# Two orders and one place of work in a two-layer transformer kernel: score matmuls of layer 0, ScalarE's and TensorE's steps of layer 1, statistics of twelve tiles

## The reference

```
ada = silu(c) @ W_ada + b_ada            # six rows: shift, scale, gate, twice
h = layernorm(x) * (1 + scale_msa) + shift_msa
x = x + gate_msa * (attention(h) @ W_proj + b_proj)
h = layernorm(x) * (1 + scale_mlp) + shift_mlp
x = x + gate_mlp * (gelu(h @ W_fc1 + b_fc1) @ W_fc2 + b_fc2)
```

## Time and profile before

| | |
|---|---|
| median of the runs | 905.08 us (904.79 to 906.73) |
| the profiled execution | 905.91 us, its span 904.1 us |
| granted TensorE clock over the span | 0.972 |
| busy, share of the span | PE 87%, DVE 72%, ACT 58%, POOL 31% |

### The profile page before, as it was taken

How to read it: one execution, slowest core, us unless ns; L and a number is a source line. 1 busy time by engine, 2 the same in 40 slices (tenths; PEclk the granted TensorE clock), 3 DMA queues, 4 the chain that set the end, 5 groups by cost and what they waited for, 6 DMA issues and landing times. The chain is left out here.

```text
span 904.1 us, 16521 instructions
## 1 busy us (share of the span) xinstructions
PE 788.5 (87%) x6096; PEld 364.0 (40%) x6096; DVE 647.4 (72%) x1277; ACT 525.0 (58%) x731; POOL 281.0 (31%) x369
## 2 busy tenths in 40 slices
PE   1568989999998989899898999999979875999996
PEld 0234222222222222222234465566646553666564
DVE  4849788888887898888935955656686898834521
ACT  4433477676676676776785725635557634535630
POOL 4320011325554241102023437241233465421122
PEclk9979799999999999999999999999999996999999
DMA  7302010110111100000040011101676710000000
GB/s 222 78 21 73 20 28 27 28 47 12 40 44 47 47 27 21 21 21 21 2 109 2 11 41 40 31 9 60 149 190 167 171 36 27 7 1 28 26 26 27
DMA packets 52127, 45.35 MB, mean 50 GB/s; under 512 B 23898, under 2 KB 41236, under 8 KB 52055
## 3 DMA queue, kind: packets, MB, share of 16 engines
q1 hardware_dynamic: 47613, 36.35, 15.7%
q10 hardware_dynamic: 4442, 8.04, 2.8%
HBM read 27.66 MB, written 9.46 MB: 41 GB/s over the span
## 5 line engine op out<-in xcount | busy, mean ns | idle before, releaser
L956 DVE TENSOR_REDUCE row_max<-ps 128x1 f32<-128x512 f32 x512 | 322.6, 686 | 62.1 <-PE ps L1682 61.2
L1445 ACT ACTIVATE probs<-ps 128x1024 f32<-128x1024 f32 x256 | 249.0, 1018 | 57.0 <-PE ps L1709 56.3
L1682 PE MATMUL ps<-stack_area 54*128 54x512 f16 x512 | 150.5, 389 | 27.9 <-DVE row_max L956 21.3
L1721 PE MATMUL ps<-probs,mlp_area 128*32 128x512 f32 x1024 | 138.0, 611 | 0.0
L1709 PE MATMUL ps<-stack_area 56*128 56x512 f16 x512 | 110.7, 385 | 7.2 <-ACT probs L1445 7.2
L1682 PEld LDWEIGHTS ps<-stack_area 54*128 54x128 f16 x512 | 37.1, 93 | 192.7 <-DVE row_max L956 174.0
L1855 PE MATMUL ps<-w_fc,mlp_area 128*128 128x288 f16 x864 | 107.7, 286 | 4.7 <-DVE mlp_area L1097 4.7
L1834 PE MATMUL ps<-mlp_area,w_fc 128*128 128x512 f16 x504 | 110.8, 379 | 0.8 <-ACT mlp_area L1486 0.8
L1486 ACT ACTIVATE mlp_area<-ps 128x512 f32<-128x512 f32 x72 | 42.8, 595 | 98.0 <-PE ps L1834 95.5
L1855 PEld LDWEIGHTS ps<-w_fc,mlp_area 128*128 128x128 f16 x864 | 83.8, 98 | 27.4 <-DVE mlp_area L1097 3.9
L765 POOL TENSOR_SCALAR neg_scaled<-neg_max 128x16 f32<-128x16 f32 x16 | 4.0, 253 | 279.8 <-DVE neg_max L963 279.8
(11 more groups left out here) (170 smaller groups left out, 1098.6 us busy)
## 6 DMA issues: line engine op xcount, KB each, us to landing
stack_area<-tokens SPq DMA_DIRECT2D x124, 36.0 KB
qkv_rows<-part_area ACTq DMA_DIRECT2D x14, 252.0 KB
qkv_rows<-probs ACTq DMA_DIRECT2D x10, 252.0 KB
x_sb<-in_x SPq DMA_DIRECT2D x4, 576.0 KB, 7.4
w_raw<-in_L_cond_W_fc SPq DMA_DIRECT2D x4, 576.0 KB
tokens<-qkv_rows SPq DMA_DIRECT2D x64, 36.0 KB
v_sb<-qkv_rows SPq DMA_DIRECT2D x16, 144.0 KB
w_raw<-in_L_cond_fc_w SPq DMA_DIRECT2D x4, 576.0 KB
```

The lines of the kernel that those rows point to most:

```text
L956: nc.vector.reduce_max(row_max[:, p % 2, t, j, half:half + 1], bank(bk), AX.X).then_inc(max_done, 1)
L1445: nc.scalar.activation(probs[:, n % 2, 2 * c:2 * c + 2, :].rearrange("p h n -> p (h n)"), ps[:, 2 + 2 * c:4 + 2 * c, :].rearrange("p b n - ...
L1682: nc.tensor.matmul(bank(bk), stacks[rows, p % RING, 0, t * P:(t + 1) * P], stacks[rows, p % RING, 1, half * 512:(half + 1) * 512], start=T ...
L1721: mm = nc.tensor.matmul(bank(6)[at:at + VW, :], v_pad[:, TB * (p // BPAIR) + n, 2 * (p % BPAIR) + j, :], probs[:, n % 2, 2 * c + j, :], st ...
```

## The change

Three things are altered.

Layer 0: in each slot TensorE follows a list, `PE_ORDER`. A P group is now cut 1-2, 3, 4-5, 6-7 and its last three pieces stand behind S1 and O: weigh, P 1-2, S0, S1, O, P 3 to 7, A, S2, B, S3. The four S steps, P and O keep their order in `plan_banks`. B's two matmuls start with the second head (`SCORE_HEADS`). The waits ahead of the first scores stand at the start of slot -1 instead of its middle.

Layer 1's attention: in ScalarE's step the columns, `high_attention` and `high_part` come before `widen` and the exponent, and the weight job before `take_rows`. In VectorE's step `invert_sums(k-1)` comes before `subtract_maxima(k)`, and `low_attention` and `turn_v` come last. In TensorE's step `out_mms` and the turned tiles come before `cell_scores`.

Statistics of layer 1's middle: those of tiles 0 to 3 stay in the steps; those of 4 to 7 stand behind step 18 between the last projections; those of 8 to 15 stand in chunk 0 of the MLP, two behind each `fc2_y`. GpSimd's `invert` follows them, and its waits on them in the steps leave.

```diff
@@ -395,6 +395,9 @@
         SCORES_FIRST = -1
+        PE_ORDER = ['W', 'P0', 'S0', 'S1', 'O', 'P1', 'P2', 'P3', 'A', 'S2', 'B', 'S3']
+        PART_RANGES = [(0, 2), (2, 3), (3, 5), (5, 7)]
+        SCORE_HEADS = [(0, 1), (1, 0)]
 
@@ -441,7 +444,8 @@
                 maxima, others = maxima_of(s), other_of(s)
-                for i, step in enumerate(part_of(s) + maxima[:2] + others + maxima[2:]):
+                order = [x for k in PE_ORDER for x in (part_of(s) if k == 'P0' else maxima[int(k[1]):int(k[1]) + 1] if k[0] == 'S' else others if k == 'O' else [])]
+                for i, step in enumerate(order):
                     now = s + i / 6
@@ -850,7 +854,8 @@
                         for t in OUT_AT.get(k - 2, ()):
-                            pool.wait_ge(rstd_ready, 3 * NT + t + 1)
+                            if t < PT_:
+                                pool.wait_ge(rstd_ready, 3 * NT + t + 1)
                         if k > 1:
@@ -860,12 +865,12 @@
                         for t in OUT_AT.get(k - 1, ()):
-                            invert(t, 3 * NT + t)
-                    for t in range(TB, NT + 2):
-                        if t < NT:
-                            add_projection(1, t)
-                        if t > TB + 1:
-                            invert(t - 2, 3 * NT + t - 2)
+                            if t < PT_:
+                                invert(t, 3 * NT + t)
+                    for t in range(TB, NT):
+                        add_projection(1, t)
+                    for t in range(PT_, TB):
+                        invert(t, 3 * NT + t)
                 stats = 2 * NT * l + NT
@@ -880,6 +885,11 @@
                 add_mlp(0)
+                if l:
+                    for t in range(TB, NT):
+                        invert(t, 3 * NT + t)
+                        if t % 2 and t < NT - 1:
+                            add_mlp(t // 2 - 3)
                 if l == 0:
@@ -889,7 +899,7 @@
                                           ).then_inc(pads_set, 1)
-                with pool.Fori(1 if l else 4, NT) as t:
+                with pool.Fori(4, NT) as t:
                     add_mlp(t)
@@ -1109,6 +1119,9 @@
                                                        fc2_bias[:], ALU.mult, ALU.add).then_inc(fc2_y, 1)
+                        if l and isinstance(c, int) and c == 0:
+                            mid_statistics(TB + 2 * i)
+                            mid_statistics(TB + 2 * i + 1)
                     if l == 0 and isinstance(c, int) and i in JOBS_AT_FC2.get(c, ()):
@@ -1180,24 +1193,25 @@
                         turn_cells(k - 2)
+                    if 0 < k <= NSTEP:
+                        invert_sums(k - 1)
                     if k < NSTEP:
                         subtract_maxima(k)
-                    if 0 < k <= NSTEP:
-                        invert_sums(k - 1)
-                    if k > 2:
-                        low_attention(k - 3)
+                    for t in OUT_AT.get(k - 1, ()):
+                        if t < PT_:
+                            mid_statistics(t)
                     for t in TILES_AT.get(k - 1, ()):
                         low_part(0, t % 2, NT + t)
                     for t in TILES_AT.get(k, ()):
                         normalise(0, t, t % 2, NT + t, 2 * NT + t, t // TB, 0)
-                    for i, a in TURN_V_AT.get(k, ()):
-                        turn_v(i, a)
-                    for t in OUT_AT.get(k - 1, ()):
-                        mid_statistics(t)
                     for t in OUT_AT.get(k, ()):
                         take_projection(1, t, t % 2, t < 2)
                     if k in JOB_STEPS:
                         low_weights(JOB_STEPS[k])
+                    if k > 2:
+                        low_attention(k - 3)
+                    for i, a in TURN_V_AT.get(k, ()):
+                        turn_v(i, a)
 
@@ -1248,10 +1262,9 @@
                             take_projection(1, TB + i - 2, i % 2, False)
-                    for t in range(TB + 2, NT + 2):
-                        mid_statistics(t - 2)
-                        if TB + 4 <= t < NT:
-                            take_projection(1, t, t % 2, False)
+                    for t in range(PT_, TB):
+                        take_projection(1, TB + t, t % 2, False)
+                        mid_statistics(t)
                 if l == 0:
@@ -1382,20 +1395,20 @@
                 for k in range(NSTEP + 3):
+                    for t in TILES_AT.get(k - 2, ()):
+                        take_columns(t, t % 2)
+                    if k > 2:
+                        high_attention(k - 3)
+                    for t in TILES_AT.get(k - 1, ()):
+                        high_part(0, t % 2, NT + t, 2)
                     if 1 < k < NSTEP + 2:
                         widen(k - 2)
                     if k < NSTEP:
                         exponents_of_cells(k)
-                    if k > 2:
-                        high_attention(k - 3)
-                    for t in TILES_AT.get(k - 1, ()):
-                        high_part(0, t % 2, NT + t, 2)
+                    if k + 1 in JOB_STEPS:
+                        high_weights(JOB_STEPS[k + 1])
                     for i, m in ROWS_AT.get(k, ()):
                         take_rows(i, m)
-                    for t in TILES_AT.get(k - 2, ()):
-                        take_columns(t, t % 2)
-                    if k + 1 in JOB_STEPS:
-                        high_weights(JOB_STEPS[k + 1])
 
@@ -1648,14 +1661,14 @@
                 for k in range(NSTEP + 2):
+                    for t in OUT_AT.get(k, ()):
+                        out_mms(t)
+                    for t in TILES_AT.get(k - 2, ()):
+                        turn(0, t % 2, NT + t, False)
                     if k + 1 < NSTEP:
                         cell_scores(k + 1)
-                    for t in TILES_AT.get(k - 2, ()):
-                        turn(0, t % 2, NT + t, False)
                     for i, m in ROWS_AT.get(k, ()):
                         rows_mms(i, m)
-                    for t in OUT_AT.get(k, ()):
-                        out_mms(t)
                     if k > 1:
@@ -1704,7 +1717,7 @@
                     pe.wait_ge(row_in, 32 * (p + 1))
-                for j in range(2):
+                for j in SCORE_HEADS[c]:
                     rows = slice(HROWS * j, HROWS * j + SR)
@@ -1754,41 +1767,42 @@
 
+            def tail_step(s):
...
             def attention():
                 for s in ALL_SLOTS:
                     maxima, part = maxima_of(s), part_of(s)
-                    if s > 0:
-                        weigh(*divmod(s - 1, SLOTS))
-                    project(part, 0, 2)
-                    side(maxima[0:1])
-                    project(part, 2, 4)
-                    side(maxima[1:2])
-                    project(part, 4, 6)
-                    side(other_of(s))
-                    project(part, 6, 7)
                     if s == SCORES_FIRST:
                         pe.wait_ge(v_ready, NT)
                         pe.wait_ge(v_padded, 1)
                         pe.wait_ge(k_ones, 32 * RING)
                         for b in range(2, 7):
                             pe.wait_ge(*freed(LAST_USERS[b]))
-                    if SCORES_FIRST <= s < NPAIR * SLOTS - 1:
-                        scores(*divmod(s + 1, SLOTS), 0)
...
-                    side(maxima[2:3])
-                    if SCORES_FIRST <= s < NPAIR * SLOTS - 1:
-                        scores(*divmod(s + 1, SLOTS), 1)
-                    side(maxima[3:4])
+                    later = SCORES_FIRST <= s < NPAIR * SLOTS - 1
+                    for step in PE_ORDER:
+                        if step == "W" and s > 0:
+                            weigh(*divmod(s - 1, SLOTS))
+                        if step[0] == "P":
+                            project(part, *PART_RANGES[int(step[1])])
+                        if step[0] == "S":
+                            side(maxima[int(step[1]):int(step[1]) + 1])
+                        if step == "O":
+                            side(other_of(s))
+                        if step in "AB" and later:
+                            scores(*divmod(s + 1, SLOTS), "AB".index(step))
+                        if step == "A" and s >= TAIL_FROM:
+                            tail_step(s)
                 weigh(NPAIR - 1, SLOTS - 1)
                 for b in SIDE_BANKS:
                     pe.wait_ge(*freed(LAST_USERS[b]))
```

More of the change, by code:

```diff
@@ L1755, in project @@
                     part_mms(*step[1:], BANK_OF[step], first, end)
+            def tail_step(s):
+                t, late = divmod(s - TAIL_FROM, 2)
+                if late:
+                    if t == 0:
+                        pe.wait_ge(*freed(LAST_USERS[1]))
+                        pe.wait_ge(w_ready, PROJ_JOBS)
+                    proj_mms(t, 1, t)
+                else:
+                    if t == 0:
+                        pe.wait_ge(*freed(LAST_USERS[0]))
+                    turn_attended(t, 0, t)
```

(19 more changed lines are left out.)

## The result

| | before | after |
|---|---|---|
| median of the runs | 905.87 us (904.79 to 906.73) | 892.15 us (889.34 to 893.41) |
| ratio, 95% interval | | 0.9833 [0.9818, 0.9848] |
| span of the profiled execution | 904.1 us | 891.4 us |

13.7 us less by the medians, where 15.6 was forecast. The page of after, for comparison with the table of before: TensorE's busy time is 781.1 us for 788.5, so 7.4 of the span's 12.7 us are busy time of TensorE and 5.3 are idle time.

What follows compares the result with a forecast made beforehand. TensorE's own list bounds layer 0's P slots, VectorE layer 1's last steps. Terms 6.3 + 1.0 + 8.3 = 15.6 us off the profiled 905.91 give 890.3; the median, 0.83 lower, 889.5; range 885.5 to 896.5.

Steps and rivals of the forecast that it cites:

- P slots: Layer 0 slots with a P group: fewer changeovers on TensorE, 0.45 us less in each of 14, 6.3 us.
- rival 2: Layer 0: S0 and S1 don't run together behind a P, only 0.23 a slot gained, 892.6 us; chance 0.10.
- Slots -12 and 0: Layer 0's ramp, same edit ahead of TensorE's steady stretch: 0.5 us less each, 1.0 together, bounds 0 to 0.9 each.
- Slots 52 and 60: Layer 0: slot 52's gain counted at nothing, since a shorter one lengthens slot 60's 2.34 us wait for a stack.
- Swapped heads: Layer 0, B's score matmuls: TensorE already takes the second head first, so 0 us; bounds 0 to 3.7.
- Rival 3: Layer 0, B: matmuls keep program order, so the head swap gives 3.7 us more, 885.8; chance 0.05.
- Layer 1, last steps: Layer 1's attention, step 9's end to step 16: bound by VectorE's own work, 3.65 us a step plus extras, 8.3 less.
- so nothing: Layer 1, ScalarE's high copy ahead of `widen`: path between values 3.2 us, under VectorE's 3.65, so 0 us.
- Rival 1: Layer 1, steps 9 to 16: TensorE or ScalarE sets them, the high copy costs 0.6 each, 894.3 us; chance 0.15.
- Rival 4: Layer 1: VectorE's sum waits for the exponent, 1.9 us in up to 16 steps, slower at 920; chance 0.05.
- Middle steps unchanged: Sign that the forecast holds: TensorE's steps in the middle of layer 1 keep their length.
- Behind it nothing is shorter: Layer 1 behind cell 15's turn: no gain, its values stay at 1.93 us; 0.85 more gained if at full clock.

Runs made afterwards that it cites:

- x8: Kernel after, with GpSimd's split of pair 9's P behind the first step of its weight job instead of the whole: 889.22 us, ratio 0.9794 to before.
- x2: Kernel before with only the second head's score matmul put first in B: 907.34 us for 907.34, ratio 1.0.
- x5: Kernel before with VectorE's new step order in layer 1 alone: 906.6 us for 906.97, ratio 1.0001.
- x3: Kernel before with the new layer 1 step orders on VectorE, ScalarE and TensorE, statistics where they were: 902.85 us for 907.34, ratio 0.9953.
- x4: Kernel before with statistics of tiles 4 to 15 later and GpSimd's waits on them gone, orders old: 905.63 us for 907.34, ratio 0.9984.
- x9: Kernel after, with the last fc2's first tile waiting for each part of its input in turn: 887.47 us, ratio 0.979 to before.
- x10: Kernel after with the edits of x8 and x9 together: 884.25 us, ratio 0.9746 to before.
- x0: Kernel after run once more unchanged, as control: 892.42 us for 907.2 of before, ratio 0.9834.
- x1: Kernel before with TensorE's new slot order in layer 0 alone, heads of B as before: 899.34 us for 907.34, ratio 0.9914.
- x11: Kernel before with VectorE's and ScalarE's new step orders together, TensorE's old: 905.44 us for 907.29, ratio 0.9978.
- x6: Kernel before with ScalarE's new step order in layer 1 alone: 905.02 us for 906.97, ratio 0.9976.
- x7: Kernel before with TensorE's new step order in layer 1 alone: 908.84 us for 906.97, ratio 1.0026.

## Why the prediction was right, and where its sizes were off

The forecast was 889.5 and the measurement 892.15, inside the range. Of the 2.65 between them 0.8 is the start: the prediction counted from a median of 905.08, and the one of the comparison is 905.87. The rest lies in the terms below.

- **P slots.** 4.33 to 3.87 in ten of the 14 slots and 4.26 to 3.83 in the other four: 6.34 for 6.3, with both pieces as worked out (S0 and S1 0.32, five P 1.23). Slots from 4 on without a P, but for 60 and 61, changed by 0.06 all together. Right, and rival 2 fell.
- **Slots -12 and 0.** 1.37 for 1.0, between the bounds, in this pair of profiles. The weigh of slot 4 lies at 107.9 to 110.3 in the eight kernels with the old slot order and at 105.4 to 107.5 in the six with the new one, and the means are 2.1 apart. So the term is sized only roughly, and 1.0 was probably low.
- **Slots 52 and 60.** Slot 52 gave 0.46 and slots 60 and 61 took 9.76 for 9.03 us. The wait itself grew to 2.97, near the 2.8 named. I had counted slot 52 at nothing; it is -0.27 net. x8 shows that the chain read at GpSimd is the cause.
- **Swapped heads.** Nothing, shown by x2. Rival 3, that program order holds, fell.
- **Layer 1, last steps.** Steps 10 to 16 took 37.40 for 43.91, 6.51 less; 5.9 was forecast (0.9 for 0.8, 0.33 for 0.1, 0.31 for 0.2, 4.98 for 4.8). Step 9's end gave 2.5 (-6.55 to -9.07), for 2.4. The turn of cell 15 comes 15.58 earlier, the forecast 15.6. That is better than the terms deserve, as the 0.9 us lost ahead of it stands against terms that were each a little small.
- **Who brings them.** Here the step of the argument was wrong, though its sum was right. I put the gain down to VectorE's order, and ScalarE's and TensorE's at nothing. That holds only for steps 14 to 16 (14.47 in x5, 14.48 with all three). The 2.5 of step 9's end come with ScalarE's order alone, and VectorE's alone lengthens that stretch by 0.9; step 10 needs both, step 11 TensorE's too. Against "so nothing" for the high copy: its earlier place is a condition of the forecast's steps 9 and 10. I had compared the two possible paths of the new kernel but not asked what VectorE's later subtraction does to the exponent and to what is queued behind that.
- **Rivals 1 and 4.** Steps 10, 14 and 15 are 3.57, 3.78 and 3.81, at VectorE's own work. Rival 1 fell for these steps. Rival 4 fell too: no sum (L1138 before) has an idle note in any profile. What x5 shows is a chain that no rival named: the late subtraction, the exponent, the high copy, the low copy, 1.2 a step beside old ScalarE. With the copy first it is gone from step 9 to step 17. In steps 5 to 8 the low copy still waits for the high copy, up to 1.50 at 692.90 (before up to 4.40 at 702.52).
- **Middle steps unchanged.** Not quite: scores of cell 0 to cell 8 take 50.44 for 49.54, and the halved clock in it lasts 6.8 us (from 659.5) for 3.4 (from 669.1). Among the kernels with step orders of before or after, 3.4 goes with 48.6 to 49.9 (before, x2, x3, x4, x9, x10) and 6.8 with 49.9 to 50.5 (after, x0, x1, x8). The two touch, so the clock is not a shown cause. There is a second candidate, which the prediction named as a sign of being wrong: TensorE waits longer on a DMA. Ahead of the scores of cells 3 and 4 it waits 1.55 and 3.22 us for `tokens<-qkv_rows` (at 654.40 and 661.12), where it was 1.10 and 3.01 (at 661.42 and 668.05), 0.66 more. Over before, x1, x2 and x4 these waits sum up to 3.8 to 5.0, over after, x0 and the three kernels on it to 4.4 to 5.1. The groups overlap, so neither is this shown to come from the new orders. And the stretch as a whole takes 48.6 to 50.5 in the latter and 49.2 to 50.2 in the former, so the 0.9 may be scatter and no effect of the change; that stays open.
- **Behind the last turn: a term I missed.** "Behind it nothing is shorter", the prediction says. It became longer: turn of cell 15 to its values is 2.15 before and 3.14 after. GpSimd's copies `widen` start beside a weight job that VectorE used to do after the low copy of cell 14 and now does before it. Timeline of after, all engines:

```profile
744.10 0.71 DVE L1162 STREAM_TRANSPOSE stack_area<-part_area 128x512 f32<-128x512 f32 x1 [1.45 <-POOL part_area L799]
744.73 1.32 DVE L1021 SCALAR_TENSOR_TENSOR w_fc<-w_raw,w_fc 128x1152 f16<-128x1152 f32 x1
744.87 2.31 POOL L811 COPY stack_area<-stack_area 32x512 f32<-32x512 f32 x2 [0.81 <-DVE stack_area L1162]
...
747.23 1.93 PE L1620 MATMUL ps<-stack_area,tokens 128*32 128x128 f32 x32 [2.71 <-POOL stack_area L811]
```

Two copies take 2.31 for 1.26: the first 1.64, where one copy took 0.60 to 0.61 in all 32 of before. It is 1.59 to 1.64 in every kernel with VectorE's new order (x3, x5, x11, after and the four on it) and 0.60 in every one without (before, x1, x2, x4, x6, x7), and the distance to the values is 3.14 in the one group and 2.12 to 2.49 in the other. The Trainium skill says that VectorE and GpSimd share a pair of ports that one instruction holds to its end, VectorE also where it has two inputs in SBUF (SBUF — State Buffer, SBUF: two separate sides); the trace agrees in the main: the weight job reads two SBUF tensors and starts 0.14 ahead of the copy, and the copy ends 0.46 behind the job's end at 746.05, where a whole copy takes 0.60. I didn't try the weight job in another place.
- **Statistics of 8 to 15.** fc2 of chunk 0 takes 13.40, that of chunk 1 13.40. Covered, as said.
- **The last fc2.** 1.67 of halved clock, in no term. The loss in the middle (0.9), the one behind the last turn (1.0) and this one are 3.6 us; without them the spans would differ by 16.3 instead of 12.7, against the forecast's 15.6. The four runs of after reach from 889.3 to 893.4, and the profiled one is the longest of them.

## What to carry to other kernels

Several orders of one pipeline belong together: an order on one engine moves a result later in its own step, and whatever is queued behind that result on the next engine pays, so read the queue behind each moved instruction on its consumer's engine, and test the parts together, not only alone. When a step is moved to the end of an engine's list, everything that it was ahead of now moves forward too; look at what another engine does at that time. A short wait of TensorE can cost more than its length, once as idle time and once as clock: taking away one of 2.97 us made its two slots 4.07 shorter. How much of that stays on the whole is another question; 1.6 of it came back further on.

## What the runs showed of the hardware

- A wait of 2.97 us in slot 60 is followed by a weigh of 1.93 us for 1.06, at half the clock. All twelve profiles with a wait there (2.34 us in before) have a halved stretch behind it, the two without it (x8, x10) have none; without it slots 60 and 61 are 4.07 us shorter.
- Behind a gap of 2.08 us TensorE ran 3.4 us at 1.2 GHz in six of twelve profiles and not in the others, with the same 108 matmuls; it costs 1.67 us.
- With slot 60's wait gone, a halved stretch of 3.4 us lay at 474.5 in x8 and x10; none of the twelve others has one there.
- Of two matmuls on different array rows, the one written second started 0.22 us ahead of the one written first in 107 of 128 slots, beside a third (S2) that stands ahead of both in the program.
- One 0.60 us copy on GpSimd took 1.64 beside a VectorE instruction of 1.32 us.
